# Attention on one core: four more key steps per head group are added on GpSimd before the row sums

## What is computed

```python
xm = xn * (1.0 + sc_a[:, None, :]) + sh_a[:, None, :]
qkv = (x @ Wqkv).reshape(b, t, 3, H, hd).transpose(2, 0, 3, 1, 4)
scores = jnp.einsum('bhqd,bhkd->bhqk', q, k) * scale
scores = jnp.where(causal, scores, -jnp.inf)
attn = jax.nn.softmax(scores, axis=-1)
out = jnp.einsum('bhqk,bhkd->bhqd', attn, v)
x = x + gt_a[:, None, :] * _attention(xm, Wqkv, Wproj, bproj)
h = jax.nn.gelu(xm @ W1 + b1, approximate=False)
x = x + gt_m[:, None, :] * (h @ W2 + b2)
```

## Time and profile before

| | us |
|---|---|
| median of 3 runs | 2285.84 (2285.28 to 2287.09) |
| the profiled execution, its own time | 2286.51 |
| its span (first to last instruction) | 2284.5 |
| PE busy | 2193.5 (96%) |
| DVE busy | 1293.9 (57%) |
| ACT busy | 935.3 (41%) |
| POOL busy | 846.0 (37%), nearly all of it within attention |

### The profile page before, as it was taken

How to read it: one execution, slowest core, us unless ns; L and a number is a source line. 1 busy time by engine, 2 the same in 40 slices (tenths; PEclk the granted TensorE clock), 3 DMA queues, 4 the chain that set the end, 5 groups by cost and what they waited for, 6 DMA issues and landing times. The chain is left out here.

```text
span 2284.5 us, 36721 instructions
## 1 busy us (share of the span) xinstructions
PE 2193.5 (96%) x11550; PEld 1463.3 (64%) x11550; DVE 1293.9 (57%) x2872; ACT 935.3 (41%) x1780; POOL 846.0 (37%) x352
## 2 busy tenths in 40 slices
PE   6999999999999899999999999889999999999998
PEld 5888884444444445444454444577888888888886
DVE  4778876776777667676776765586323133133132
ACT  2111115555556555555555566444422222222221
POOL 2001008667578575785757773581000000000000
PEclk9999999999999999998999999999999999999999
DMA  6547446234261442614326231585211011010010
GB/s 228 208 154 254 145 160 148 48 90 103 53 136 46 92 91 53 149 39 98 79 53 149 50 88 52 181 286 201 92 56 56 0 55 55 0 55 30 25 37 18
DMA packets 129287, 223.46 MB, mean 98 GB/s; under 512 B 8526, under 2 KB 26006, under 8 KB 128920
## 3 DMA queue, kind: packets, MB, share of 16 engines
q1 hardware_dynamic: 107992, 179.38, 28.8%
q10 hardware_dynamic: 21120, 41.95, 5.0%
HBM read 146.31 MB, written 74.98 MB: 97 GB/s over the span
## 5 line engine op out<-in xcount | busy, mean ns | idle before, releaser
L1172 ACT ACTIVATE prob<-st 128x512 f32<-128x512 f32 (+3 forms) x1280 | 613.1, 544 | 431.1 <-PE st L1346 416.4
L1142 POOL TENSOR_TENSOR psum_k<-psum_k,prob 128x2048 f32<-128x2048 f32 x122 | 550.4, 4512 | 42.1 <-ACT prob L1172 34.7
L1228 DVE TENSOR_REDUCE part<-mx 128x1 f32<-128x512 f32 x708 | 435.8, 683 | 132.9 <-PE mx L1326 132.8
L1346 PE MATMUL st<-q_st,k_st 98*128 98x512 f32 (+3 forms) x1280 | 489.2, 397 | 16.5 <-issue 9.0
L1326 PE MATMUL mx<-k_st,qx_st 96*128 96x512 f32 (+3 forms) x1188 | 470.2, 415 | 18.6 <-DVE part L1224 13.3
L1346 PEld LDWEIGHTS st<-q_st,k_st 98*128 98x128 f32 x1280 | 245.7, 193 | 203.8 <-issue 115.5
L1740 DVE TENSOR_TENSOR m_g_lo<-m_g,m_g_hi 128x512 fp32r<-128x512 f32 x128 | 88.7, 693 | 495.3 <-ACT m_g_hi L1654 495.2
L1326 PEld LDWEIGHTS mx<-k_st,qx_st 96*128 96x128 f32 x1188 | 227.1, 192 | 169.2 <-DVE part L1228 96.9
L1224 DVE CUSTOM_DVE_ANT_0 unused<-mx,mask_row 128x128 bf16<-128x128 f32 x480 | 214.0, 488 | 148.7 <-PE mx L1326 131.5
L1363 PE MATMUL o_ps<-prob,v_sb 128*32 128x512 f32 (+3 forms) x2560 | 292.9, 564 | 0.0
L1650 ACT ACTIVATE m_g<-m_hid,vcol 128x512 f32<-128x512 f32 x128 | 88.3, 690 | 480.6 <-PE m_hid L1837 480.6
(11 more groups left out here) (168 smaller groups left out, 2608.1 us busy)
## 6 DMA issues: line engine op xcount, KB each, us to landing
k_st<-qk_scratch SPq DMA_DIRECT2D x96, 256.0 KB, 8.1
qx_st<-qk_scratch SPq DMA_DIRECT2D x96, 256.0 KB, 4.7
q_st<-qk_scratch SPq DMA_DIRECT2D x96, 256.0 KB
qk_scratch<-st_hi ACTq DMA_DIRECT2D x16, 1024.0 KB, 4.2
qk_scratch<-st_lo ACTq DMA_DIRECT2D x16, 1024.0 KB, 6.8
xs<-in_x_dram SPq DMA_DIRECT2D x8, 1024.0 KB, 8.4
v_sb<-v_scratch SPq DMA_DIRECT2D x8, 1024.0 KB, 15.8
o_scratch<-o_sb SPq DMA_DIRECT2D x32, 256.0 KB, 2.3
```

The source lines that it names most:

```text
L1142: nc.gpsimd.tensor_tensor(dst, src, prob[:, s % BUF, :, m:], ALU.add).then_inc(pool_added, 1)
L1172: nc.scalar.activation(prob[:, s % BUF, h, m:], st[n % RING][:, m:], ACT.Exp, scale=SCALE).then_inc(exp_done, 1)
L1228: nc.vector.tensor_reduce(most, bank[:, 0:w], AX.X, ALU.max).then_inc(mx_free, 1)
L1346: nc.tensor.matmul(st[n % RING][:, m:], k_st[u][0:MROWS, h, kt * P:(kt + 1) * P], q_st[0:MROWS, pos % 2, h, m:], start=True, stop=True).th ...
```

## The change

In the table `POOLED` chunk 3 gets the steps 3 and 11, chunk 2 the step 3 and chunk 1 the step 5. These four steps are no longer direct: PE's ones matmuls of line 1370 go, and POOL has an add for each. The last group's table stays as it is.

```diff
@@ class Plan
-    POOLED = {3: (0, 1, 2, 4, 5, 6, 8, 9, 10, 12), 2: (0, 1, 2, 4, 5, 6, 8, 9), 1: (0, 1, 2, 4), 0: ()}
+    POOLED = {3: (0, 1, 2, 3, 4, 5, 6, 8, 9, 10, 11, 12), 2: (0, 1, 2, 3, 4, 5, 6, 8, 9), 1: (0, 1, 2, 4, 5), 0: ()}
     POOLED_LAST = {3: (0, 1, 2, 4, 5, 6, 8, 9, 10, 12), 2: (0, 1, 4, 7), 1: (), 0: ()}
```

## The result

| us | before | after |
|---|---|---|
| median, executions taken side by side | 2285.56 (4; 2284.68 to 2287.09) | 2258.52 (4; 2255.48 to 2263.47) |
| profiled execution: own time, span | 2286.51, 2284.5 | 2256.66, 2254.9 |
| PE busy | 2193.5 | 2164.5 |
| POOL busy | 846.0 | 965.2 |

The ratio is 0.9882, 95% interval 0.9868 to 0.9895: the change takes 27.0 us off. The prediction was 2265, with a range from 2260 to 2277.

What follows compares the result with a forecast made beforehand. PE, 96% busy, was taken as the bound, its score parts going at DVE's pace. Ones products of 22.6 us less 1.2 and 6 x 0.05 gave 21.1 off 2286.5, less 0.7 for the median: 2265 us, range 2260 to 2277.

Steps and rivals of the forecast that it cites:

- The ones products (22.6 us): PE in seven groups: three ones products of 0.86 us and one of 0.65 removed per group, 22.6 us in all.
- The cover by DVE's idle time: Behind each removed ones product DVE idles 1.8 us or more, covering 0.86; idle time drops from about 2.2 to 1.3.
- The walk of POOL's queue: Adds and masks of chunk 3, group 2, followed in order: mask of step 13 done at 676.8, first add at 629.17.
- PE's arrival: When PE reaches product 13 in chunk 3: 676.7 to 677.6, so its mask is 0.1 us late or 0.8 early.
- The term of 0.05 us for each of six groups: Allowance taken off the gain in the groups after the first, 6 x 0.05 us; 0.3 us per group the bad end.
- The bound of 2268 us: Slow end from the terms alone: waits of 0.3 us in each of six groups and 1.7 in the first.
- The first group (1.2 us): Chunk 3 of the first group: late mask of step 13 and late exponentials of step 17, together 1.2 us off.
- a late exponential of step 17: First group, chunk 3: ACT's exponentials of step 17 wait some 1 us for POOL's add of step 12.
- a low stretch of the clock or two fewer: Reason given for the range's low end of 2260 us: one or two fewer stretches of PE at half clock.
- Rival (c): Less dense PE work brings more half-clock stretches: 2300 us in full, chance 0.07; 2277 in mild form, chance 0.06.
- Rival (b): Mask of step 13 about 3 us later per group, as with adds of 4.95 us: 2286 us; chance 0.09 with mixtures.
- (a): POOL becomes what chunk 3 waits for, so 1.72 us per group are lost: 2275 us, chance 0.16.

Runs made afterwards that it cites:

- e_c2: The kernel before with only step 3 of chunk 2 pooled in addition: 2279.70 us, 0.9971.
- e_c21: The kernel before with only step 3 of chunk 2 and step 5 of chunk 1 pooled in addition: 2271.91 us, 0.9943.
- e_c3: The kernel before with only steps 3 and 11 of chunk 3 pooled in addition: 2275.04 us, 0.9948.
- e_bunched: The changed kernel with step 7 of chunk 3 pooled in place of step 12: 2282.55 us, 0.9985 of the kernel before.

## Why the prediction was right, and where it failed

**The ones products (22.6 us): right.** Blocks are shorter by 0.85 or 0.86 us at the two places measured at full clock, for step 5 the 0.64 between `e_c2` and `e_c21` bears out the 0.65 taken by width, and at equal time at half clock the seven groups are 22.2 us shorter. The 11.9 us of `e_c3` say less: its interval is 6.6 us wide.

**The cover by DVE's idle time: right.** 1.32 us is left where 1.3 was said.

**The walk of POOL's queue: right to 0.1 us** in the changed kernel, and the same walk to 0.2 in the bunched one. PE's arrival was the less certain half: "0.1 us late or 0.8 early" became 1.2 early. Since the granted clock is at half there, product 13 starts 1.7 us after product 12, near the later of the two ends that I had given. The term of 0.05 us for each of six groups measured 0. (The bound of 2268 us beside the sum is mis-added: waits of 6 x 0.3 and 1.7 us give 2267.) The groups themselves did not shrink evenly, by 2 us for the first and 3.2 for the others, but by 1.8 and by 2.5 to 4.9 in the means of the traces, since the stretches at half clock moved.

**The first group (1.2 us): too much.** POOL in order of time:

```profile
351.58 4.57 POOL L1142 TENSOR_TENSOR psum_k<-prob 128x2048 f32<-128x2048 f32 x1
356.30 37.64 POOL L1142 TENSOR_TENSOR psum_k<-psum_k,prob 128x2048 f32<-128x2048 f32 x8
```

The pitch is 4.70, as assumed, and the mask of 13 ends at 399.62, 48.0 us after the first add; I had said 48.1. PE starts product 13 at 399.77, 1.98 us after product 12 where the other groups have 1.71 or less: a wait of 0.27 us. The 1.2 us held a late exponential of step 17 too, for which no loss shows in PE's rows, and PE comes later than I had it, since its clock is low there for 6.8 us in all four traces (3.4 in two of the three of before, none in the third). So the small wait is partly luck: in `e_c3`, with full clock at that place, PE waits 1.86 us, more than the 0.8 that the walk had. The half clock slows the products and hides the late mask.

**The clock: the step that failed.** I wrote the range's low end as "a low stretch of the clock or two fewer", and took all else as fixed. The sum had no term for the clock in attention, whose net effect is -1.6 us: the seven groups shrink by 23.9 in the means of the traces, and the ones products less the wait of 0.27 give 22.3. The 3.4 us less at half clock (68.3 to 64.9) are worth 1.5 us at the 3 us for 6.8 of above, an estimate that fits. It had no term for the part behind the seven groups, 1.7 us shorter in the mean (949.9 to 948.1; the highest of four traces of after is 948.6, the lowest of three of before 949.0). Whether that is the change's isn't shown: over all the kernels of this case, with all but the same work in that part, it goes from 947.5 to 950.9. And it took three executions of the kernel before that lie within 1.8 us of each other as the measure of the spread, where ten of the changed kernel go from 2255.5 to 2263.5 (median 2259.3, four of them above 2260), partly by the draw of 3 us ahead of attention, and those of before in the later jobs from 2280.3 to 2289.5. The prediction's miss of 6.5 us is thus 0.9 + 0.3 (the waits), 1.6 (clock in attention), 1.7 (behind it), and 2.0 that are left over and that I put down to the draw. A low end at 2255 would have been the honest one.

**Rival (c) was real, but small.** The low stretches did get longer at the end of chunk 3, by 13 us in all. They got shorter by 19 elsewhere, 17 of it within the groups, and I had only asked for more of them. The Trainium skill, TensorE: Matmul & The Clock Gate, section on psum-queue depth-cycling, which tells of short idle times that make the clock swing, fits what the traces of both kernels show (PE is busy for 2.45 of the 3.40 us before the clock falls). That less dense work would make it swing more isn't borne out, since 68.3 us at half clock within the groups became 64.9.

**Rival (b)** has no support: the adds take 4.5 to 4.6 us, one every 4.65. Of the Trainium skill, GPSIMD Engine Reference, the 4497 ns of section 3.1 are near the 4.5 to 4.6 us measured, but the queue goes by the pitch. Section 4.1 would keep such adds on VectorE. No run here puts them there; what the runs show is that 28 of them more on GpSimd come with a gain of 27 us, where next to nobody waits for it. **(a)** needed POOL's masks to be what PE waits for, and they were 1.2 us early. `e_bunched` shows how near POOL is to being the bound of chunk 3: one more add ahead, 4.64 us, takes nearly all the gain, more through ACT's wait for a buffer than through PE's for a mask (9.5 and 6.4 us of PE's idle time). The prediction had that wait of ACT in its walk, but only for steps 16 and 17.

**Open.** Why a low stretch lasts 3.4 or 6.8 us; why a chunk 2 that is shorter by 0.86 us settles it a chunk later; and what the 1.7 us behind the seven groups are, if they are more than draw.

## What to carry to other kernels

An engine that is idle on average can take work from the bound one, even at five times the price (4.64 us of POOL for 0.86 of PE), if each addition is placed in its queue by the time at which someone needs what stands behind it; walk the queue instruction by instruction and for every engine that waits on it, since one add more ahead of the masks turned a gain of 27 us into one of 3, and PE waited more for ACT, which waited for a buffer, than for the masks. A gain of this size is a sum of many small equal ones, so it can be checked to 0.02 us on a block at full clock, while the total carries a few us of clock. Before two totals are compared, see whether they had the same time at half clock. Give the range of a prediction the spread of the executions, and take that from more than three of them.

## What was not expected of the hardware

- The length of a low-clock stretch at one place went with the length of the work a chunk before it: 6.8 us in 23 of 42 groups with the one chunk 2, in 0 of 63 with a chunk 2 shorter by 0.86 us. At half clock 3.4 us more cost 1.2 us at the end of chunk 1, and 6.8 us more cost 3 us of the seven groups.
- One execution differs from the next by a stretch of half clock near 40 us of the span (granted clock 0.93 or 1.00 from 25 to 48 us), and is about 3 us later when attention begins.
- An add of 2048 columns on POOL keeps its pitch of 4.64 to 4.70 us with POOL at nine tenths busy and DVE at 7 tenths beside it: the denser use slowed neither (DVE is busy for 693.7 and 693.3 us of the seven groups).
- In the changed kernel the half clock at the end of chunk 3 hides a late mask in the first group: PE's wait is 0.27 us with it, and 1.86 us in the run that has full clock there.
